# A one-core transformer block: other banks and orders for the first two groups, and the last group's second matmul by halves

## What is computed

```python
x_norm = _layer_norm(x, ln1_w, ln1_b)
Q = jax.nn.elu(_linear(x_norm, q_w, q_b)) + 1.0      # 64 features
K = jax.nn.elu(_linear(x_norm, k_w, k_b)) + 1.0
V = _linear(x_norm, v_w, v_b)
attn = _causal_linear_attn(Q, K, V)                  # running sums over the 512 rows
x = x + _linear(attn, o_w, o_b)
h = jax.nn.gelu(_linear(_layer_norm(x, ln2_w, ln2_b), f1_w, f1_b), approximate=False)
x = x + _linear(h, f2_w, f2_b)
```

## Time and profile before

| | |
|---|---|
| median of 3 runs | 489.58 us (488.97 to 490.57) |
| the profiled execution | 487.23 us, its span 485.5 us |
| TensorE busy | 455.8 us, 94% of the span, 3058 matmuls |
| VectorE | 379.1 us, 78% |
| ScalarE | 326.1 us, 67% |
| GpSimd | 135.3 us, 28% |
| mean granted clock of TensorE | 0.975 |

### The profile page before, as it was taken

One profiled execution on the slowest core, in us unless ns is written; L12 is line 12 of the kernel. 1 busy time (PEld: TensorE's weight loads), 2 busy tenths in 40 slices (PEclk: granted clock), 3 DMA queues, 4 the chain that ended last, 5 costly groups with the idle time before them and its releaser, 6 DMA issues.

```text
span 485.5 us, 8738 instructions
## 1 busy us (share of the span) xinstructions
PE 455.8 (94%) x3058; PEld 413.8 (85%) x3058; DVE 379.1 (78%) x995; ACT 326.1 (67%) x611; POOL 135.3 (28%) x132
## 2 busy tenths in 40 slices
PE   4785999989999999999999999999999999989796
PEld 3684888878998899889989999989989989879686
DVE  4677858886799769976898769977899688884576
ACT  3776973869458965799358955799458954864262
POOL 2274204322053113512252203602261021520300
PEclk9877999999999999999999999999999999999889
DMA  7221000100001000100010000100020000000001
GB/s 260 120 93 38 1 0 1 45 22 2 1 23 44 23 1 23 45 22 1 2 56 11 23 1 23 45 23 0 2 65 24 1 2 22 2 22 1 24 0 45
DMA packets 10043, 14.08 MB, mean 29 GB/s; under 512 B 784, under 2 KB 9104, under 8 KB 9488
## 3 DMA queue, kind: packets, MB, share of 16 engines
q1 hardware_dynamic: 10000, 13.52, 8.2%
HBM read 9.32 MB, written 4.19 MB: 28 GB/s over the span
## 4 chain that ended last, share of the span: by engine, by line
PE 69%; DVE 12%; issue 10%; POOL 3%; ACT 3%; DMA 0%; DVEq 0%; POOLq 0%; ACTq 0%
PE bank_f L367 9%; PE bank_p L397 9%; PE bank_y L178 6%; PE bank_y L179 5%; PE bank_y L180 5%; PE bank_f L178 5%; PE bank_f L179 5%; PE bank_f L180 5%; PE bank_y L381 4%; PE bank_a L178 3%; PE bank_a L180 3%; PE bank_a L179 3%; PE bank_a L186 2%; DVE sh L789 2%; DVE g_lo L933 2%
## 5 line engine op out<-in xcount | busy, mean ns | idle before, releaser
L1036 POOL TENSOR_TENSOR rs<-ve,neg_half 128x2 f32<-128x2 f32 x48 | 33.7, 703 | 196.2 <-DVE ve L784 195.6
L178 PE MATMUL bank_y<-wf_hi,h_hi 128*128 128x256 f32 x256 | 72.1, 282 | 1.0 <-DVE h_lo L811 1.0
L179 PE MATMUL bank_y<-wf_lo,h_hi 128*128 128x256 f32 x256 | 71.5, 279 | 0.0
L180 PE MATMUL bank_y<-wf_hi,h_lo 128*128 128x256 f32 x256 | 71.4, 279 | 0.0
L623 ACT ACTIVATE g_hi<-bank_y,vec 128x256 fp32r<-128x256 f32 x128 | 53.5, 472 | 19.6 <-PE bank_y L381 18.0
L811 DVE TENSOR_TENSOR h_lo<-bank_f,h_hi 128x512 fp32r<-128x512 f32 x64 | 43.9, 688 | 28.3 <-ACT h_hi L593 27.5
L397 PE MATMUL bank_p<-wpj_t,g_hi 128*128 128x256 f32 x256 | 64.9, 289 | 0.2 <-DVE y_yc L942 0.2
L397 PE MATMUL bank_p<-wpj_t,g_lo 128*128 128x256 f32 x256 | 62.6, 279 | 0.0
L933 DVE SCALAR_TENSOR_TENSOR g_lo<-bank_y,vec,g_hi 128x256 fp32r<-128x256 f32 x128 | 55.0, 476 | 5.6 <-ACT g_hi L623 5.0
L367 PE MATMUL bank_f<-wfc_t,z3T_hi 128*128 128x512 f32 x128 | 54.5, 426 | 0.6 <-DVE z3T_lo L811 0.5
L178 PE MATMUL bank_f<-z2T_hi,wf_hi 128*128 128x512 f32 x128 | 52.7, 412 | 1.4 <-DVE z2T_lo L811 1.4
(11 more groups left out here) (166 smaller groups left out, 1180.0 us busy)
## 6 DMA issues: line engine op xcount, KB each, us to landing
x_sb<-in_x SPq DMA_DIRECT2D x16, 256.0 KB, 2.8
out<-y_yc SPq DMA_DIRECT2D x16, 256.0 KB, 2.1
h<-in_f SPq DMA_DIRECT2D x1, 1024.0 KB, 7.6
y_yc<-in_f SPq DMA_DIRECT2D x1, 1024.0 KB, 9.5
h<-in_fc SPq DMA_DIRECT2D x1, 1024.0 KB, 11.5
h<-in_pj SPq DMA_DIRECT2D x1, 1024.0 KB, 4.7
z<-in_wv SPq DMA_DIRECT2D x1, 256.0 KB, 3.9
z<-in_wo SPq DMA_DIRECT2D x1, 256.0 KB, 4.0
```

The lines of the kernel that those rows point to most:

```text
L178: pe.matmul(ps, w[0], r[0], start=start, stop=False, skip_group_check=skip)
L179: pe.matmul(ps, w[0], r[1], start=False, stop=False, skip_group_check=skip)
L180: return pe.matmul(ps, w[1], r[0], start=False, stop=stop, skip_group_check=skip)
L1036: pool.tensor_tensor(rs[n][:, 2 * h:2 * h + 2], ve[n][:, 2 * h:2 * h + 2], neg_half[:, 0:2], ALU.pow).then_inc(s[f"ln{n + 1}_rs"], 1)
```

## The change

- Banks: attention of group 0 uses the banks of f1, fc and proj (f0, f1, p) through a_bank, and its V matmul bank_y through v_bank. Attention of group 1 starts beside it in its own banks. The matmuls of the weights' preparation move to the other banks.
- v_mm(0, .) comes ahead of the scores and waits for u_lo and not for ae_lo and af_lo. f1b waits for v_lo. theta_sum and threshold are done in two parts, one for each weight.
- Two buffers for x (x_two); the load of x of group 1 is issued ahead of the loads of f2 and fc. The sums of |W| write their unused output to g_hi's memory.
- In the last group the second matmul is done by halves h (f2h), half 0 ahead of half 1, with y_sum(7, h) after its half; the tiles m = 4 to 7 of h_hi and h_lo go to memory of the attention that is no longer used (h_tile), and so don't wait for f2.
- The written order is another one on all four engines, in first(), step(g) and last().

The core of the diff (of ScalarE's first() only the new order; of last() only parts):

```diff
+        def a_bank(g, i):
+
+            return (bank_a[0], bank_a[1], bank_q)[i] if g else (bank_f[0], bank_f[1], bank_p)[i]
+
+        def v_bank(g, h):
+
+            return bank_a[h] if g else bank_y[h]
+
+        def h_tile(part, g, m):
+
+            if g < G - 1 or m < RH:
+                return hr[part][:, (8 * g + m) % RH, :]
+            return ((uT[0][:, 0, :], uT[0][:, 1, :], uT[1][:, 0, :], uT[1][:, 1, :]),
+                    (q_stack[:], k_stack[:], ad[0][:], ad[1][:]))[part][m - RH]
...
-        x_sb = sb("x_sb", [P, T, D])
+        x_two = [sb("x_even", [P, T, D]), sb("x_odd", [P, T, D])]
...
             sp.dma_start(f1_raw, f1_d).then_inc(s["f1_loaded"], 16)
+            load_x(1)
             sp.dma_start(f2_raw, f2_d).then_inc(s["f2_loaded"], 16)
             sp.dma_start(fc_raw, fc_d).then_inc(s["fc_loaded"], 16)
             sp.wait_ge(s["wf1_lo"], 4)
             sp.wait_ge(s["f1b_done"], 1)
             sp.dma_start(pj_raw, pj_d).then_inc(s["pj_loaded"], 16)
-            load_x(1)
...
             def v_mm(g, h):
-                pe.wait_ge(s["ae_lo" if h == 0 else "af_lo"], g + 1)
-                if g == 0:
+                if g:
+                    pe.wait_ge(s["ae_lo" if h == 0 else "af_lo"], g + 1)
+                else:
+                    pe.wait_ge(s["u_lo"], h + 1)
                     pe.wait_ge(s["wvo_lo"], 2)
                 for j in range(2):
                     t = 2 * h + j
                     for k in range(KD):
-                        mm = split3(bank_a[h][:, j * D:(j + 1) * D], [r[:, k, t * P:(t + 1) * P] for r in uT],
+                        mm = split3(v_bank(g, h)[:, j * D:(j + 1) * D], [r[:, k, t * P:(t + 1) * P] for r in uT],
...
+            def f2_part(g, k, h):
+                pe.wait_ge(s["h_lo"], 8 * g + k + 1)
+                for t in (2 * h, 2 * h + 1):
+                    mm = split3(bank_y[h][:, (t % 2) * D:(t % 2 + 1) * D],
+                                [h_tile(part, g, k)[:, t * P:(t + 1) * P] for part in range(2)],
+                                [w[:, k, :] for w in wf2], k == 0 and t % 2 == 0, k == KH - 1, skip=True)
+                return mm
...
+            def f2h(g, k, h):
+
+                if k == 0:
+                    pe.wait_ge(s["g_lo"], 16 * (g - 1) + 14 + 2 * h)
+                f2_part(g, k, h).then_inc(s[f"f2_half{h}"], 1)
...
             def first():
 
-                qkb(); wvo_mm(); tu(0, 0); tu(0, 1); qk_mm(0); bvo(); f1b(); scores(0); v_mm(0, 0); v_mm(0, 1)
-                attend(0, 0); attend(0, 1); attend(0, 2); attend(0, 3); theta_sum(); tz2(0, 0); tz2(0, 1); f1(0, 0)
-                f1(0, 1); tu(1, 0); f1(0, 2); f2(0, 0); tu(1, 1); f1(0, 3); f2(0, 1); qk_mm(1); f2(0, 2); f1(0, 4)
-                f1(0, 5); cpj(); f2(0, 3); spread(); f2(0, 4); f1(0, 6); scores(1); f1(0, 7); f2(0, 5); f2(0, 6)
-                f2(0, 7); v_mm(1, 0); v_mm(1, 1); attend(1, 0); attend(1, 1); tz3(0, 0); attend(1, 2); attend(1, 3)
-                tz3(0, 1); fc(0, 0, 0); fc(0, 0, 1); fc(0, 1, 0); fc(0, 1, 1); tr(0, 0, 0); fc(0, 2, 0); tr(0, 0, 1)
-                tz2(1, 0); fc(0, 2, 1); fc(0, 3, 0); proj(0, 0, 0); tr(0, 0, 2); tz2(1, 1); fc(0, 3, 1); tr(0, 0, 3)
-                proj(0, 0, 1); tr(0, 1, 0)
+                qkb(); wvo_mm(); tu(0, 0); tu(0, 1); bvo(); v_mm(0, 0); qk_mm(0); v_mm(0, 1); f1b(); scores(0)
+                attend(0, 0); attend(0, 1); attend(0, 2); attend(0, 3); tu(1, 0); theta_sum(0); tu(1, 1); tz2(0, 0)
+                tz2(0, 1); qk_mm(1); f1(0, 0); f1(0, 1); theta_sum(1); f1(0, 2); f1(0, 3); f2(0, 0); f2(0, 1)
+                f1(0, 4); f2(0, 2); f1(0, 5); f2(0, 3); cpj(); f1(0, 6); spread(); scores(1); f2(0, 4); f1(0, 7)
+                f2(0, 5); f2(0, 6); f2(0, 7); v_mm(1, 0); v_mm(1, 1); attend(1, 0); attend(1, 1); tz3(0, 0)
+                attend(1, 2); fc(0, 0, 0); tz3(0, 1); attend(1, 3); fc(0, 0, 1); fc(0, 1, 0); fc(0, 1, 1)
+                tr(0, 0, 0); tr(0, 0, 1); fc(0, 2, 0); fc(0, 2, 1); tr(0, 0, 2); proj(0, 0, 0); fc(0, 3, 0)
+                tz2(1, 0); proj(0, 0, 1); tz2(1, 1); tr(0, 0, 3); fc(0, 3, 1); tr(0, 1, 0)
 
             def step(g):
 
-                proj(g - 1, 0, 2); f1(g, 0); f1(g, 1); tu(g + 1, 0); tr(g - 1, 1, 1); proj(g - 1, 0, 3)
-                tr(g - 1, 1, 2); f1(g, 2); proj(g - 1, 1, 0); tr(g - 1, 1, 3); f1(g, 3); f1(g, 4); f2(g, 0)
-                tu(g + 1, 1); f2(g, 1); f1(g, 5); qk_mm(g + 1); f2(g, 2); f1(g, 6); f1(g, 7); f2(g, 3); f2(g, 4)
-                f2(g, 5); f2(g, 6); f2(g, 7); scores(g + 1); proj(g - 1, 1, 1); proj(g - 1, 1, 2); v_mm(g + 1, 0)
-                proj(g - 1, 1, 3); tz3(g, 0); v_mm(g + 1, 1); attend(g + 1, 0); attend(g + 1, 1); tz3(g, 1)
-                fc(g, 0, 0); attend(g + 1, 2); fc(g, 0, 1); fc(g, 1, 0); attend(g + 1, 3); tr(g, 0, 0); fc(g, 1, 1)
-                tr(g, 0, 1); fc(g, 2, 0); tr(g, 0, 2); fc(g, 2, 1); fc(g, 3, 0); tz2(g + 1, 0); proj(g, 0, 0)
-                proj(g, 0, 1); fc(g, 3, 1); tz2(g + 1, 1); tr(g, 0, 3); tr(g, 1, 0)
+                proj(g - 1, 0, 2); tu(g + 1, 0); f1(g, 0); f1(g, 1); proj(g - 1, 0, 3); tr(g - 1, 1, 1)
+                tr(g - 1, 1, 2); tu(g + 1, 1); proj(g - 1, 1, 0); f1(g, 2); tr(g - 1, 1, 3); f1(g, 3); qk_mm(g + 1)
+                f2(g, 0); f2(g, 1); f1(g, 4); f2(g, 2); f1(g, 5); f2(g, 3); f1(g, 6); f1(g, 7); scores(g + 1)
+                f2(g, 4); f2(g, 5); f2(g, 6); f2(g, 7); v_mm(g + 1, 0); proj(g - 1, 1, 1); v_mm(g + 1, 1)
+                proj(g - 1, 1, 2); proj(g - 1, 1, 3); attend(g + 1, 0); tz3(g, 0); attend(g + 1, 1); tz3(g, 1)
+                attend(g + 1, 2); fc(g, 0, 0); attend(g + 1, 3); fc(g, 0, 1); fc(g, 1, 0); fc(g, 1, 1); tr(g, 0, 0)
+                fc(g, 2, 0); tz2(g + 1, 0); fc(g, 2, 1); tr(g, 0, 1); fc(g, 3, 0); tr(g, 0, 2); proj(g, 0, 0)
+                fc(g, 3, 1); proj(g, 0, 1); tr(g, 0, 3); tz2(g + 1, 1); tr(g, 1, 0)
 
             def last():
...
+                proj(6, 1, 0); f1(7, 4); f2h(7, 0, 0); tr(6, 1, 3); f1(7, 5); f2h(7, 1, 0); f2h(7, 2, 0)
+                f2h(7, 3, 0); f1(7, 6); f2h(7, 4, 0); f1(7, 7); f2h(7, 5, 0); f2h(7, 0, 1); f2h(7, 6, 0)
+                f2h(7, 1, 1); f2h(7, 7, 0); f2h(7, 2, 1); f2h(7, 3, 1); f2h(7, 4, 1); f2h(7, 5, 1); f2h(7, 6, 1)
+                f2h(7, 7, 1); proj(6, 1, 1); tz3(7, 0); proj(6, 1, 2); proj(6, 1, 3); fc(7, 0, 0); tz3(7, 1)
...
                 act.wait_ge(s["h_gelu"], 8 * g + m + 1)
-                if 8 * g + m >= RH:
+                if g == G - 1 and m >= RH:
+                    act.wait_ge(s["v_done"], 2 * G)
+                elif 8 * g + m >= RH:
                     act.wait_ge(s["f2_done"], 8 * g + m - RH + 1)
-                act.activation(hr[0][:, (8 * g + m) % RH, :], bank_f[m % 2][:], ACT.Copy).then_inc(s["h_hi"], 1)
+                act.activation(h_tile(0, g, m), bank_f[m % 2][:], ACT.Copy).then_inc(s["h_hi"], 1)
...
+                wqk_hi(); u_norm(0, 0); u_norm(0, 1); ln3_hi(); wvo_hi(); u_hi(0, 0); u_hi(0, 1); n1(0); v_hi(0, 0)
+                wf1_hi(0); qk_exp(0); wf1_hi(1); qk_hi(0); v_hi(0, 1); eps_split(); wf1_hi(2); wf2_hi(0); wf1_hi(3)
+                ae_hi(0); af_hi(0); ad_hi(0); u_norm(1, 0); wf2_hi(1); u_norm(1, 1); wf2_hi(2); abs_part(0)
+                abs_part(1); wf2_hi(3); u_hi(1, 0); z2_norm(0, 0); u_hi(1, 1); z2_norm(0, 1); z2_hi(0, 0)
+                z2_hi(0, 1); abs_part(2); abs_part(3); gelu(0, 0); h_hi(0, 0); gelu(0, 1); h_hi(0, 1); gelu(0, 2)
+                h_hi(0, 2); gelu(0, 3); h_hi(0, 3); qk_exp(1); gelu(0, 4); h_hi(0, 4); gelu(0, 5); qk_hi(1); rows()
+                n1(1); gelu(0, 6); h_hi(0, 5); af_hi(1); h_hi(0, 6); ae_hi(1); spread_copy(); ad_hi(1); gelu(0, 7)
+                h_hi(0, 7); v_hi(1, 0); v_hi(1, 1); z3_norm(0, 0); z3_hi(0, 0); z3_norm(0, 1); u_norm(2, 0)
+                z3_hi(0, 1); gelu3(0, 0, 0); gelu3(0, 0, 1); gelu3(0, 1, 0); gelu3(0, 1, 1); g_hi(0, 0, 0)
+                g_hi(0, 0, 1); gelu3(0, 2, 0); z2_norm(1, 0); z2_norm(1, 1); gelu3(0, 2, 1); g_hi(0, 0, 2)
+                z2_hi(1, 0); gelu3(0, 3, 0); z2_hi(1, 1); gelu3(0, 3, 1); g_hi(0, 0, 3)
...
+                consts(); ln1_stats(0); qk_bias_add(); ln1_shift(0); wide_cols(); ln3_lo(); wqk_lo(); wvo_lo()
+                u_lo(0, 0); u_lo(0, 1); bo_rows(); qk_max(0); v_lo(0, 0); ln1_stats(1); qk_sum(0); wf1_lo(0)
+                wf1_lo(1); qk_lo(0); ln1_shift(1); v_lo(0, 1); eps_lo(); wf1_lo(2); ad_mask(0); ae_lo(0); af_lo(0)
+                ad_lo(0); wf1_lo(3); attn_out(0, 0); ln2_stats(0, 0); attn_out(0, 1); ln2_stats(0, 1)
+                attn_out(0, 2); ln2_var(0, 0); ln2_stats(0, 2); attn_out(0, 3); ln2_stats(0, 3); ln2_shift(0, 0)
+                ln2_var(0, 1); f1_bias_add(); ln2_shift(0, 1); u_lo(1, 0); threshold(0); u_lo(1, 1); z2_lo(0, 0)
+                z2_lo(0, 1); ternary(0); h_lo(0, 0); qk_max(1); h_lo(0, 1); threshold(1); ternary(1); h_lo(0, 2)
...
-                g_lo(g - 1, 0, 3); g_lo(g - 1, 1, 0); h_lo(g, 0); output(g - 1, 0); g_lo(g - 1, 1, 1); h_lo(g, 1)
```

(40 more changed lines are left out.)

## The result

The changed kernel takes 492.39 us (median of 7 runs, 491.78 to 493.46), the kernel before 489.58 beside it (7 runs, 488.74 to 490.57): ratio 1.0072, 95% interval 1.0054 to 1.0089. It is slower by 0.7%, by the mechanism of the forecast. The span of the profiled execution is 490.2 us, 4.7 above that of before.

What follows compares the result with a forecast made beforehand. TensorE bounds the kernel, its middle full, so only the ends can win: 2.3 + 1.6 + 1.0 + 1.8 + 3.0 = 9.7 us won, 13.4 lost to waits, net +3.7 on the 489.58 median: 493.3 us, range 481 to 498.

Steps and rivals of the forecast that it cites:

- the mechanism of the forecast: Middle steps: GpSimd adds starting with VectorE's shift and corrections hold VectorE up, and TensorE waits twice per step.
- the forecast case: Both waits recur in each of five steps: net +3.7 us, 493.3 us, own range 488 to 498, chance 0.50.
- the head: Start of the kernel, group 0: 2.3 us won at the fronts, 1.6 by the g_lo wait going in step 1.
- last(): End of the kernel: 1.0 us (h_lo(6,7) wait), 1.8 (g_lo wait) and 3.0 (tail by halves) won.
- The two waits per step: TensorE waits for g_lo at a step's start and h_lo in its middle: 1.65 + 1.03 us, 13.4 lost over five.
- The walk: Working through the new order with today's durations: waits of 1.6 us for g_lo and 1.4 for h_lo.
- Three such places, all outside the middle: Earlier trace: VectorE held up beside GpSimd adds following an rstd only there, with TensorE waits of 1.63, 1.03, 1.65 us.
- R1: Rival: one of the two waits per step has slack; net -1.5 or -4.5 us, 485 to 488, chance 0.20.
- R2: Rival: VectorE is over 2.8 us ahead at both corrections, TensorE's middle stays full; net -9.7, 479.9 us, chance 0.20.
- my own mark for a mis-sized head: Head: f1(0,2), the third first-matmul tile, starting at 48.8 us or later, or scores after 25.
- Two edits that I put at nothing: Two x buffers, and own memory for f2's tiles 4 to 7 of the last group: each said to win nothing.
- The rule of the Trainium skill: VectorE's second read port is shared with GpSimd and held for a whole instruction; without it, 9.7 us faster than before.

Runs made afterwards that it cites:

- the head alone: Kernel before with the changed first() and two x buffers, old step(), last() and ring of four for h: 483.77 us, ratio 0.9897.
- short adds: Changed kernel, orders untouched, n1o, xpb and xs of groups 2 to 6 adding only 8 of 256 columns, sums incomplete: 476.08 us, ratio 0.9740.
- the run with the corrections moved: Changed kernel, GpSimd untouched, each VectorE correction of the middle one place later, behind h_lo(g,7) or g_lo(g-1,0,3): 488.34 us, ratio 0.9993.
- the run with three adds cut: Changed kernel, orders untouched, GpSimd's n1o, xpb and xs each cut into adds of 128 columns of one tile: 478.36 us, ratio 0.9773.
- the best version: Changed kernel, orders untouched, all of GpSimd's wide adds (n1o, xpb, xs and y_cpj) cut into four: 476.50 us, ratio 0.9733.

## Why the prediction was right

Forecast 493.3, measured 492.39, by the forecast case. Set against the spans, the head wins 3.3 us (the head alone, above), last() 7.3, and five steps lose 15.4: +4.8, where the spans differ by 4.7. The prediction had 3.9, 5.8 and 13.4. A gain and a loss were too small by 1.5 and 2.0 us and nearly cancelled, which is luck; the head was too large by 0.6. A second piece of luck: the net of 3.7 was set on the median of before, and the medians differ by 2.8. The spans differ by 4.7 because the profiled execution of before, 487.23 us, was faster than all seven that were timed beside the changed kernel. By medians and ratios the head wins 5.0 and last() 6.6.

- **The two waits per step**, taken from the earlier trace rows as 1.65 + 1.03, show as 1.42 and 1.23 and cost 1.58 and 1.50. In place of 2.7 us a step loses 3.08 against before. The term was mis-sized because I read a wait's price off its idle time; the matmuls that start behind it cost 0.2 to 0.3 us more each. (Against short adds a step loses 3.37: the steps of before lose 0.3 to y_cpj.) The places, the causes, the shift of 1.25 and the corrections of 1.87 and 2.91 are as written.
- **The walk** of the order gave 1.6 and 1.4 for the same two waits, and was nearer than the rows that I preferred.
- **"Three such places, all outside the middle"** is a misreading. The shift beside y_cpj(g) takes 1.2 us in every step of the middle before, as shown above. It cost those steps 0.3 us, so a step with TensorE busy for 53.90 of 53.92 us was not one in which nothing could be won. The new VectorE order has v_lo(g+1,0) ahead of that shift and doesn't pay it.
- **R1 and R2** fell as both waits came out in full, in each of the five steps. That VectorE is busy for 48 of 57 us did not help it: at these two places it is only 0.6 and 1.2 us ahead, and is held up for 2.1 and 2.8 (the run with the corrections moved).
- **The head.** Scores 24.69 (24.1 forecast), attention from 30.11 (29.8) to 35.8 (35.4): right to 0.6 us, with the clock back 3 us after the start. But f1(0,0) starts at 44.22, not 43.0, and f1(0,2) at 49.07, not 48.0; my own mark for a mis-sized head was 48.8. z2_lo is done at 43.22. The step that failed: I counted qk_mm(1) as work already done, 1.4 us at full clock, ahead of f1(0,0); it runs in the clock's low stretch behind the two waits for z2 and takes 2.70:

```profile
40.75 1.12 PE L206 MATMUL bank_f<-ident,z 128*128 128x128 f32 x4 [1.86 <-ACT z L549]
41.52 0.78 PE L198 MATMUL bank_a<-uT_hi,wqk_hi 128*128 128x512 f32 x1
...
44.22 0.63 PE L198 MATMUL bank_f<-z2T_hi,wf_hi 128*128 128x512 f32 x1
```

  So the head at f1(0,2) is 0.3 us late where I had it 0.8 early. What it wins comes later: the work done ahead, and waits for v_lo, z3 and g_lo of 3.1 us in all (0.5 + 0.5 + 0.5 + 1.6) of which 1.2 are left (0.5 + 0.7). Of these I had only the 1.6, and took it as gone in full; 0.7 stays.
- **last().** With F = 460.50, fc(7,0,1) starts at F + 7.5 (7.1 forecast), with pauses of 1.16 and 1.41 (1.1 and 1.4). The clock stays up, which I had left open at 0.9 us: from F to the end it is 29.7 us against 33.35, 3.6 won where I took 3.0. The rest, 1.0 + 1.8, measured 7.3 - 3.6 = 3.7; part of it is the price of the starts again. But that the clock stays up is luck of this execution. With the same last(), six of the nine profiled executions have a stretch at half clock around the second pause, 3.4 us long in five and 6.8 in one. From F to the end it is then 30.4 to 31.3 us and 32.5, so against 33.35 the tail wins 2.1 to 3.0 (the 3.0 with y_cpj cut as well) or 0.8. The longest, of the run with three adds cut:

```profile
444.28:476.79 32.51, 26.07 (x162) 22.63 (x160) 22.19 (x56) 13.59 (x29) 4.63 (x5) 0.90 0.07 25
```

- **Two edits that I put at nothing** do win nothing by themselves, but the others can't be had without them. The memory of f2's tiles 4 to 7: with the ring of four, h_hi(7,4) waits for both halves of tile 0, and the second half of tile 0 stands behind the first half of tile 4, which needs h_hi(7,4). The second x buffer: GpSimd's new order stops without it, as told with the run of that order above. Both are read from the code, and neither was tried without its memory.
- **The rule of the Trainium skill** ("SBUF — State Buffer", "Who interferes with whom") held, and it was the larger part of the sum. The runs add to it that the stall is as long as what is left of one add: the shift takes 1.25 us beside adds of 1.29 and 0.42 beside adds of 0.46.

Still open: what decides whether a pause is followed by a stretch at half clock, and with it 1.3 to 2.8 us of the time of the last() that is common to nine of these runs.

## What to carry to other kernels

Before an add is placed on GpSimd, look at what VectorE starts in the same moment: an rstd or another short result of GpSimd releases VectorE just when GpSimd's next instruction begins, so nothing long should stand directly behind it. A row without idle time doesn't clear such a place: look for a short VectorE instruction that lasts far longer than its like elsewhere. If the order can't be kept free of that, cut the long instruction: here four small adds in place of one took GpSimd 48% longer and won 8 us in the old kernel and 16 in the new one. And price a wait from start to start of the same two instructions in two traces, not by the idle time of its row.

## What the runs showed of the hardware

- Not only instructions with two inputs in SBUF stand still. In the run with GpSimd's old step, a tensor_scalar on 128x4 numbers, one tensor and two constants, lasts 1.27 us beside the second add of xs, and its neighbour, ahead of that add, 0.17:

```profile
141.17 0.17 DVE L846 TENSOR_SCALAR ve<-mv 128x4 f32<-128x4 f32 x1
141.25 1.27 DVE L847 TENSOR_SCALAR ve<-mv 128x4 f32<-128x4 f32 x1
...
139.94 2.55 POOL L1126 TENSOR_TENSOR y_yc<-y_yc,xa 128x512 f32<-128x512 f32 x2
```

  g_lo, with one input in PSUM, keeps its 0.47 us each beside xs (changed kernel, 155.35 us). bn_stats keeps its 0.41 each beside xpb and xs (four at 139.26 us in the run with GpSimd's old step, 1.40 in all, as in the earlier trace rows). The Trainium skill has a rule for the first of these: on "VectorE: DVE Perf Modes", "Mode 2×_2P — use both read ports for one tensor", a tensor_scalar or tensor_copy whose one tensor lies in SBUF can read it through both read ports at once. The trace agrees with it, 1.27 us against 0.17.
- A short pause can be followed by a stretch at half clock (1.2 in place of 2.4 GHz), and the same pause isn't always. Of the five waits of 2.2 to 2.3 us in the run with GpSimd's new order in the kernel before, three were followed by 3.4 us of it, which costs a step 1.64 us, and two were not; nor was the 2.51 us of the run with all four steps as before. The 1.65 us for g_lo in the old last() was followed by one in two of four traces. Single waits of 1.2 and 1.4 us in the steps never were. In the tail the pair of 1.16 and 1.41 (0.33 and 1.41 in the best version), about 2 us apart, had such a stretch at or behind its second wait in six of nine. What decides, no run here tells.
